# Context attentions of a decoder: one PSUM bank from the ring of turned scores to the ring of scores

## What is computed

```
H = 16; d_k = D // H
q, k, v = proj(x, Wq, bq), proj(ctx, Wk, bk), proj(ctx, Wv, bv)   # b, H, 512 or 154, 8
scores = einsum('bhqd,bhkd->bhqk', q, k) / sqrt(d_k)              # where masked: a large negative number
p = softmax(scores, axis=-1)
x = layernorm(x + einsum('bhqk,bhkd->bhqd', p, v) @ Wo + bo)
```

## Time and profile before

| | us |
|---|---|
| median of 3 runs | 3139.39 |
| lowest, highest | 3135.52, 3140.32 |
| the profiled execution | 3138.19 |
| its span, first to last instruction | 3136.5 |
| TensorE busy (15420 matmuls) | 2668.2, 85% |
| VectorE busy | 2038.3, 65% |
| ScalarE busy | 1339.2, 43% |
| mean granted TensorE clock | 0.922 of 2.4 GHz |

### The profile page before, as it was taken

The page is one execution under the profiler, slowest core; times in us unless marked ns, Lnnn a source line. Parts: engine busy times, 40 slices in busy tenths (PEclk is TensorE's granted clock), DMA queues, the critical chain, the costliest instruction groups (busy, mean ns, idle before and its releaser), DMA issues. The chain is left out here.

```text
span 3136.5 us, 43700 instructions
## 1 busy us (share of the span) xinstructions
PE 2668.2 (85%) x15420; PEld 1238.6 (39%) x15420; DVE 2038.3 (65%) x5373; ACT 1339.2 (43%) x2298; POOL 997.8 (32%) x1254
## 2 busy tenths in 40 slices
PE   6997869987875988898988999978864999798998
PEld 1332424433322442354563444444432232354555
DVE  6885861259997756666784666656576887573444
ACT  2664742265552652221213434425641567463221
POOL 3212100068896101333433554553045110200000
PEclk9998979989887989999999999998875999899999
DMA  5321400000002400122230000003000221330000
GB/s 117 70 37 25 94 21 1 0 0 0 1 1 48 113 11 10 37 52 56 51 72 20 1 1 1 1 11 61 14 0 18 49 44 27 72 68 1 4 4 7
DMA packets 52134, 95.66 MB, mean 30 GB/s; under 512 B 14966, under 2 KB 36266, under 8 KB 46462
## 3 DMA queue, kind: packets, MB, share of 16 engines
q1 hardware_dynamic: 50620, 90.39, 13.7%
q10 hardware_dynamic: 1296, 2.47, 0.3%
HBM read 46.20 MB, written 1.38 MB: 15 GB/s over the span
## 5 line engine op out<-in xcount | busy, mean ns | idle before, releaser
L1955 POOL TENSOR_TENSOR mamba_dbu<-mamba_du,mamba_b 128x512 f32<-128x512 f32 x128 | 246.1, 1923 | 40.7 <-DVE mamba_du L2009 12.6
L1988 DVE TENSOR_TENSOR_SCAN stream<-mamba_da,mamba_dbu 128x512 f32<-128x512 f32 x128 | 215.8, 1686 | 17.4 <-issue 8.8
L1699 PE MATMUL ps<-stream,weights 128*128 128x512 f32 x256 | 151.9, 701 | 61.2 <-DVE stream L1998 44.1
L2843 DVE CUSTOM_DVE_ANT_0 ps<-ps,bconst 128x512 f32<-128x512 f32 (+3 forms) x256 | 119.3, 511 | 115.9 <-PE ps L2670 115.9
L664 DVE TENSOR_REDUCE L3a_negmax<-ps 128x1 f32<-128x512 f32 x256 | 162.5, 683 | 40.6 <-PE ps L368 40.2
L664 DVE TENSOR_REDUCE L0a_negmax<-ps 128x1 f32<-128x512 f32 x256 | 162.4, 683 | 38.6 <-PE ps L368 38.1
L485 ACT ACTIVATE L0a_probs<-ps 128x512 f32<-128x512 f32 x256 | 143.9, 599 | 70.9 <-PE ps L387 69.4
L485 ACT ACTIVATE L3a_probs<-ps 128x512 f32<-128x512 f32 x256 | 143.9, 599 | 68.9 <-PE ps L387 67.4
L2906 ACT ACTIVATE skv_probs<-ps 128x1024 f32<-128x1024 f32 (+3 forms) x128 | 90.2, 704 | 175.5 <-PE ps L2695 175.5
L165 POOL TENSOR_SCALAR vareps<-mv 128x4 f32<-128x4 f32 x24 | 8.9, 370 | 486.9 <-DVE mv L1429 486.7
L190 PE MATMUL ps<-stream,xT 128*64 128x512 f32 x512 | 128.8, 621 | 14.5 <-DVE moa_v L2446 7.3
(11 more groups left out here) (666 smaller groups left out, 6503.0 us busy)
## 6 DMA issues: line engine op xcount, KB each, us to landing
moa_masks<-picked SPq DMA_DIRECT2D x32, 512.0 KB, 6.7
stream<-stream SPq DMA_DIRECT2D x28, 192.0 KB
stream<-gate_up_down_in SPq DMA_DIRECT2D x16, 272.0 KB, 3.4
stream<-value_output_in SPq DMA_DIRECT2D x16, 256.0 KB, 3.4
pre<-gates SPq DMA_DIRECT2D x32, 128.0 KB
stream<-ffn_in SPq DMA_DIRECT2D x16, 180.5 KB, 3.1
pre<-pre SPq DMA_DIRECT2D x40, 64.0 KB
L0a_qs<-L0a_qs SPq DMA_DIRECT2D x16, 128.0 KB
```

Source lines behind the costliest of these rows:

```text
L1699: pe.matmul(ps[:, SUM_BANK + j, :], k.ident, hc[:, (J * i + j) % RING, :], start=n == 0, stop=n == N - 1).then_inc(s["summed"], 1)
L1955: pool.tensor_tensor(dbu[:, m % RING, :], du[:, b % 2, j, :], bsb[:, i % B_RING, :], ALU.mult).then_inc(s["dbu_ready"], 1)
L1988: dve.tensor_tensor_scan(out=hs[:, m % RING, :], data0=da[:, m % RING, :], data1=dbu[:, m % RING, :], initial=0.0, op0=ALU.mult, op1=ALU.a ...
L2843: last = dve.tensor_tensor_reduce(ps[:, bank + a, 0:n], ps[:, bank + a, 0:n], later[:, SEQ - n:], -1.0, 3e38, ALU.add, ALU.min, negmax[:, ...
```

## The change

In `cross_attention` alone, the ring of scores becomes three banks (0 to 2) and the ring of turned scores two (3 and 4). The scratch tile `masked`, which VectorE writes beside each maximum in the masked stages, gets three slots in place of two. No instruction is added, removed or moved; the operands and two constants in waits differ. The self attentions keep their own constants.

```diff
@@ cross_attention
-    S_RING, T_BANK, T_RING, Z_BANK, A_BANK, B_BANK = 2, 2, 3, 5, 6, 7
+    S_RING, T_BANK, T_RING, Z_BANK, A_BANK, B_BANK = 3, 3, 2, 5, 6, 7
...
-            masked = sb("masked", [P, 2, 2, CTX], BF16)
+            masked = sb("masked", [P, S_RING, 2, CTX], BF16)
...
-                            last = dve.tensor_tensor_reduce(masked[:, i % 2, p, :], at, mask_q[:, hh // H % 2, 2 * u + p, :], -1.0, 3e38, ALU.add,
+                            last = dve.tensor_tensor_reduce(masked[:, i % S_RING, p, :], at, mask_q[:, hh // H % 2, 2 * u + p, :], -1.0, 3e38, ALU.add,
                                                             ALU.min, negmax[:, hh // G % 4, 2 * u + p, hh % G:hh % G + 1])
```

## The result

The changed kernel takes **3176.56 us** (median of 4 runs, 3169.33 to 3182.0) against 3137.45 for the kernel before on the same chip (4 runs, 3132.66 to 3140.32): ratio **1.0125**, 95% interval 1.01 to 1.015, some 39 us more. The forecast was 3183 in a range of 3158 to 3210. The profiled execution of after is the slowest of its four runs, 3182.0 with a span of 3180.3, so its own differences add up to 43.8 us.

The account below looks back on a forecast made before the run. TensorE was taken as the bound wherever scores and exponentials run side by side, except in L0x's VectorE stretches. Groups 41.8 plus ends 9.5 less 6 for the third bank gave +45.3 on 3138.2, so 3183 us (range 3158 to 3210).

Parts of the forecast that it names:

- the groups: Two-step groups that TensorE bounds, all four stages: 1.15 us lost each unmasked, 0.64 masked, 41.8 us in all.
- the ends: Last five steps of a stage, without scores between: 3 us in L2x, 2.9 each masked, 0.7 in L0x, 9.5 in all.
- the third bank: Extra bank for scores: 6 us gained or absorbed, 2 at stage starts, 1 in VectorE stretches, 3 in rest of L0x.
- the VectorE stretches of L0x: Where VectorE bounds L0x: no loss counted for later turned scores, about 1 us gained from the third bank.
- mid-stage stop: ScalarE idle 5.40 us in L2x: hides losses of one or two groups, 1.5 us, stretch left out of the count.
- The path of a bank: Turned score to reuse of its bank: 0.47 to exponential, 0.59 exponential, 0.05 to load, 0.11 to matmul, 1.22 us.
- first stall: Turned score 2 in a group's first step waits for exponential 0: 0.52 us unmasked, 0.31 masked.
- second stall: Turned score 2 in a group's second step, z's copy ahead of its exponential: 0.68 us unmasked, 0.33 masked.
- Stages: Loss by stage: L2x some 17 us, L0x, L1x and L3x 10 to 12 each.
- What would show it: Signs of being right: L2x loads waiting 25 to 30 times, 0.4 to 0.7 us each; fewer waits on maxima everywhere.
- the fall of the clock: Rival: small holes in TensorE's work cost its full clock, +24 us more, 3207, up to 3230; chance 0.13.
- The fast case: Rival: the third bank of scores pays, 9.4 us of waits on maxima could go, 3129 us; chance 0.05.

Follow-up runs that it names:

- rings_2_2: The changed kernel with the ring of scores back at two banks and one bank left unused; 3174.09 us, ratio 1.0119 to the kernel before.
- after_again: The changed kernel as it is, measured a second time beside the kernel before; 3176.41 us, ratio 1.0125.
- before_bias: The kernel before, with GpSimd adding the output bias to x three steps later; 3129.49 us, ratio 0.9976 to the kernel before.
- after_bias: The changed kernel, with GpSimd adding the output bias to x three steps later; 3166.39 us, ratio 1.0087 to the kernel before.
- weigh_first: The changed kernel with the weighing of the step before moved ahead of turned score 2 in TensorE's loop; 3141.97 us, ratio 1.0018 to the kernel before.

## Why the prediction was right, point by point

The sign and the mechanism came out as forecast, and the sum within 6 us: +45 predicted, +39 measured. Part of that nearness is luck: the groups, the ends and the third bank at the starts came out 14.5 us below my terms, and the VectorE stretches of L0x 7.4 us above theirs, and 3 us that I had taken off in the rest of L0x had no waits under them. The terms fared like this; the measured ones are sums of step lengths of after less those of before, us:

```
                                  predicted                         measured in after
                                  L0x   L1x   L2x   L3x    sum      L0x   L1x   L2x   L3x    sum
groups of two steps               10.8   8.3  14.1   8.6   41.8      9.2   6.8  11.5   6.7   34.2
steps without scores (ends)        0.7   2.9   3.0   2.9    9.5     -0.2   2.0   2.3   2.0    6.1
up to the first exponential       -0.5  -0.5  -0.5  -0.5   -2.0     -1.6  -1.2  -1.5  -1.2   -5.5
VectorE stretches, mid-stage stop -1.0   0.0   0.0    -    -1.0      6.4  -0.4   0.0    -     6.0
waits on maxima, rest of L0x      -3.0    -     -     -    -3.0      0.0    -     -     -     0.0
rest (first weighing, output)       -     -     -     -      -       0.6  -0.4  -1.0  -1.0   -1.8
all                                                         45.3    14.4   6.8  11.3   6.5   39.0
```

- **The path of a bank.** Turned score to exponential 0.48 (0.47 predicted), exponential 0.59, end to next load 0.05: all as read from the earlier trace rows. The step that was off is the last 0.11: after a wait the matmul starts with its load (2189.21 and 2189.22), not 0.11 behind it. So a first stall costs 0.43 where I had 0.52, and turned score 2 of the second step comes 1.24 after turned score 0 where it came 0.70 before. The second stall, 0.54, was 0.68 in my sum. Masked, the loads show 0.23 us idle, and a regular group grows by 0.49 (7.97 to 8.46), where I had 0.64.
- **The groups.** In the 8 regular groups of L0x (I had counted 9.4) a group lost 1.15 us, 9.2 in all; 1.15 is what I had taken. In L2x it was 0.96 over 12 groups, in good part because steps 9 to 13 were already longer in before (3.40 to 3.84 us) and lost 0.37 us each. In L1x and L3x it was 0.57 and 0.52. The 1.15 came right for a reason that I did not have. The two stalls of a group are 0.43 and 0.54, 0.97 where I had 1.20. But where nothing stands between the steps, turned score 1 of the second step waits as well (0.20 us idle at 2184.39), and so a step of 2.77 and one of 2.94 both become 3.51. I had put that wait down as nearly covered.
- **The ends.** 2.0 to 2.3 us a stage in place of 3, and nothing in L0x.
- **The third bank.** Up to the first exponential it gave 5.5 us, more than the 2 I had taken there. But the step as I put it, 6 us gained or absorbed, failed as a mechanism: rings_2_2, without the bank, is as fast. What it gains at the starts goes again later, in L0x and L1x by after, in L0x, L1x and L2x by after_again. And the 3 us that I took off for waits on maxima in the rest of L0x have nothing under them: in the trace of before all such waits of L0x lie at its start (3.6 us) or in its VectorE stretches (6.0 at 352 to 363, 3.0 at 386 to 393).
- **The VectorE stretches of L0x.** I counted nothing for later turned scores and a gain of 1 us. The ten steps in the two stretches took 6.4 us more in after, 4.0 in after_again and 2.4 in rings_2_2. This is the term that was wrong in sign. 2.4 us are there with two banks of scores and no more half clock than before; what is above that comes with more half clock and the third bank, not parted.
- **The mid-stage stop.** I took 1.5 us of loss as hidden by it and left that stretch out of the count. The stretch of two steps was even in after (13.17 to 13.19 us) and 14.79 in after_again, and before_bias and after_bias, with the stop halved or less, are 37 us apart, as before and after are within the intervals. Left out was right, hidden was not shown.
- **Stages.** I said some 17 us for L2x and 10 to 12 for the others; for L0x that doesn't follow from my own terms, which give 7.0. L2x lost 11.3 (14.0 in after_again), L0x 14.4 (11.5), the masked ones 6.8 and 6.5. That L0x would lose as much as L2x I had named as a sign of being wrong, and in after it lost more; rings_2_2, with 10.6 in L0x and 12.3 in L2x, has the shorter ring alone as the cause of most of it. The masked stages are the ones I had too high in every term.
- **What would show it.** Loads waiting 25 to 30 times in L2x for 0.4 to 0.7 us: 41 times against 7 before. 28 of the 41 come while scores still run, 0.48 on average, and before had none there; the other 13, and the 7 of before, lie in the last steps, where matmuls run during most of such a gap. Waits on maxima down in all four: yes. Clock the same in the regular stretches: 0.99 and 1.00 before, 1.00 after.

Of the rivals, the fall of the clock is ruled out for the regular groups by the windows at 1.00, and with it what the Trainium skill says in "TensorE: Matmul & The Clock Gate", section "A second HAM failure mode: psum-queue depth-cycling": the pattern of idles between groups is there in after (14.59 of 16 us busy), the swing of the clock is not. The fast case was the rule of the Trainium skill, "Perfetto Trace Analysis", section "Optimization Strategy", that a gap repeating on the engine that should be saturated can mean too few buffers in PSUM. It does describe after: the gap repeats at the turned scores, once a step, and a third buffer closes it (3137 against 3174 us for rings_2_2). The gaps of before, on maxima, did shrink by 9.1 us with one more bank, but the time did not. That this is near the 9.4 I had named is chance: I meant the waits outside the starts, and 5.5 of the 9.1 are at the starts.

## What to carry to other kernels

Before a bank is moved between rings, write down for each ring the path of one bank, from write through read to release (here 0.48 + 0.59 + 0.05 = 1.12 us), and compare it with the distance at which the in-order engine comes back to that bank (in steps with scores 0.70 us at its shortest with two banks, 1.3 to 1.5 with three: in before turned score 3 at 2156.33 and turned score 2 of the next step at 2157.63, or 2162.50 and 2163.98). Add what the reader does in between: with z's copy ahead of the exponential the path is 1.24. The ring must be longer than the path; the bank beyond that only moved waits about here. Where the bank is missing, look first for independent long work of the same engine to put between two uses of it: moving a weighing of 1.06 us gave back 34 of 39 us at no bank at all. And where an in-order queue waits long, look at what stands behind the head of it: GpSimd is not the bound, but in the last 8 of the 26 us that it waited in L2x, work that TensorE needed stood ready behind the head; reordering its loop took 9 us off the whole.

## What the runs showed of the hardware that I had not expected

- A matmul that was held up by a semaphore starts within 0.01 us of its weight load (2189.21 and 2189.22), while one in a running stream started 0.11 behind it, others 0.06 to 0.07 (2183.61 and 2183.68 in after).
- Repeated holes of 0.2 to 0.4 us before matmuls (0.4 to 0.6 before their loads), two or three in 7.37 us, left TensorE's granted clock at 1.00 over 16 and 31 us of L2x. In L0x of after it was 0.71 in a window in which TensorE was busy 5.25 of 8 us, and 0.52 in the next, in which it was busy all 8.
- The idle time in the row of a weight load is not lost time where matmuls run meanwhile: 0.84 us before the load at 2164.28 in weigh_first, none before its matmul.
- The same program spent 34.9 us of the middle part of L0x at 1.2 GHz in one execution and 24.6 in another, and L0x differed by 2.9 us; a difference of a few us in that stage needs more than one trace.
